# Half of a convolution inside the last units of the stage before it, a weight tile cleared in pieces, and eight input loads in advance

## What is computed

```python
x = x + einsum('bct,bcd->bdt', x, W0[condition])       # step 0, a 64x64 matrix per sample
x = x + conv1(x) * (t < len1[b])                       # step 1, causal, length 1024, per channel
x = x + x @ weight.T + bias + scale * lora(x)          # step 2, 1024x1024 over time, rank-16 adapter per sample
x = x + conv3(x * (t < len3[b])) * (t < len3[b])       # step 3, causal, as step 1
# the kernels of both convolutions: K[h, l] = 2 Re sum_n Ct[h, n] exp(dtA[h, n] * l)
```

## Time and profile before

| | us |
|---|---|
| median of three timed runs | 1580.62 |
| lowest and highest of them | 1577.86, 1584.58 |
| the profiled execution | 1581.37 |
| its span in the trace | 1579.6 |
| granted TensorE clock, mean | 0.984 |

### The profile page before, as it was taken

One profiled execution on the slowest core, in us unless ns is written; L12 is line 12 of the kernel. 1 busy time (PEld: TensorE's weight loads), 2 busy tenths in 40 slices (PEclk: granted clock), 3 DMA queues, 4 the chain that ended last, 5 costly groups with the idle time before them and its releaser, 6 DMA issues.

```text
span 1579.6 us, 36811 instructions
## 1 busy us (share of the span) xinstructions
PE 1496.6 (95%) x14983; PEld 1296.4 (82%) x14983; DVE 1238.7 (78%) x1478; ACT 744.0 (47%) x1084; POOL 636.6 (40%) x452
## 2 busy tenths in 40 slices
PE   6787777899999999999999999999999999999998
PEld 6687775778888888888888888888888888888887
DVE  7887757879696969696969787878878796969653
ACT  4544443345454545454535454545444444545433
POOL 2111122775444453535353535354545454545030
PEclk9999988999999999999999999999999999999999
DMA  7799985748493848567675747474849484848432
GB/s 226 274 356 381 360 332 174 173 94 224 93 222 98 210 118 193 135 173 155 153 175 132 196 116 201 109 206 110 215 89 231 88 227 82 234 94 224 101 134 68
DMA packets 437911, 283.43 MB, mean 179 GB/s; under 512 B 330568, under 2 KB 377168, under 8 KB 437776
## 3 DMA queue, kind: packets, MB, share of 16 engines
q1 hardware_dynamic: 388560, 172.47, 46.2%
q10 hardware_dynamic: 49216, 108.88, 19.9%
HBM read 159.20 MB, written 73.86 MB: 148 GB/s over the span
## 4 chain that ended last, share of the span: by engine, by line
PE 74%; DVE 9%; DMA 6%; issue 4%; ACT 3%; POOL 3%; ACTq 1%; DVEq 0%; POOLq 0%
PE ps L935 35%; PE ps L838 8%; PE ps L1023 6%; PE ps L944 5%; PE ps L911 5%; PE ps L882 4%; PE ps L1036 3%; DMA arena<-in_x_dram 3%; PE ps L848 3%; DVE arena L1839 3%; PE ps L786 3%; DMA w_scratch<-gbuf 1%; DVE gbuf L1834 1%; ACT arena L1380 1%; ACT arena L1287 1%
## 5 line engine op out<-in xcount | busy, mean ns | idle before, releaser
L935 PE MATMUL ps<-arena,w2t 128*128 128x256 f16 x4608 | 523.3, 273 | 5.9 <-DMA w2t<-w_scratch 4.7
L935 PEld LDWEIGHTS ps<-arena,w2t 128*128 128x128 f16 x4608 | 451.5, 98 | 62.8 <-DMA w2t<-w_scratch 5.0
L641 POOL TENSOR_TENSOR arena<-arena 128x68 f32<-128x68 f32 x31 | 26.6, 859 | 685.2 <-DVE arena L1889 394.1
L1932 DVE TENSOR_TENSOR arena<-arena 128x512 f16<-128x512 f32 x128 | 111.1, 869 | 115.8 <-ACT arena L1369 115.8
L786 PE MATMUL ps<-arena 128*128 128x128 f32 x1024 | 141.6, 300 | 44.0 <-DMA arena<-in_x_dram 23.5
L786 PEld LDWEIGHTS ps<-arena 128*128 128x128 f32 x1024 | 133.3, 212 | 50.1 <-DMA arena<-in_x_dram 27.1
L1356 ACT ACTIVATE arena<-ps,biasx 128x256 f32<-128x256 f32 x256 | 103.5, 472 | 137.0 <-PE ps L935 99.6
L1827 DVE SCALAR_TENSOR_TENSOR arena<-gbuf,arena 128x1024 f16<-128x1024 f32 x64 | 162.9, 2565 | 1.6 <-ACT arena L1283 1.6
L1369 ACT ACTIVATE arena<-arena 128x512 f16<-128x512 f32 x128 | 80.6, 630 | 163.3 <-DVE arena L1928 157.9
L882 PE MATMUL ps<-arena 128*128 128x512 f16 (+1 forms) x768 | 137.8, 330 | 7.8 <-DVE arena L1827 7.8
L1023 PE MATMUL ps<-arena 128*128 128x256 f16 (+1 forms) x1536 | 137.1, 246 | 1.9 <-DVE gbuf L1834 0.8
(11 more groups left out here) (255 smaller groups left out, 2777.9 us busy)
## 6 DMA issues: line engine op xcount, KB each, us to landing
w2t<-w_scratch ACTq DMA_DIRECT2D x96, 512.0 KB, 4.1
arena<-in_x_dram SPq DMA_DIRECT2D x64, 512.0 KB, 8.4
out_dram<-arena SPq DMA_DIRECT2D x64, 512.0 KB, 3.2
gbuf<-x_scratch SPq DMA_DIRECT2D x60, 512.0 KB, 5.6
x_scratch<-arena ACTq DMA_DIRECT2D x28, 960.0 KB, 11.0
gbuf<-w_scratch ACTq DMA_DIRECT2D x32, 512.0 KB, 4.2
arena<-krow_scratch SPq DMA_DIRECT2D x31, 512.0 KB, 8.5
arena<-tab_scratch SPq DMA_DIRECT2D x62, 68.0 KB, 2.2
```

Source lines behind the costliest of these rows:

```text
L935: mm = nc.tensor.matmul(ps[:, bank, n * HW:(n + 1) * HW], weight(p, n, part, k), xx[:, :, k], start=(fresh and n == 0 and k == 0 and q == ...
L1932: tt(x3_quarter(x3l, h0, row), x3part[slot].rearrange("p (k h b) -> p k h b", k=2, h=2), x3_quarter(x3h, h0, row), ALU.subtract).then_inc( ...
```

## The change

Stage 0's last units take in work of group 0's step 1. The input of blocks 0 to 3 (the first half of the times) is complete after unit 3; it is split in unit 6, and `near1` of the first half runs for the four heads in steps 4 to 7 of unit 7. Tables and bases of group 0 are made earlier, in new places. The rest of group 0's convolution is done by halves in another order. The opening clears `pick` in eight pieces on two engines, changes the order of loads, and loads eight x tiles ahead instead of four. The diff, cut:

```diff
+        x_ahead = area(104, 16).rearrange("p (s n t) -> p s n t", s=NXIN, n=GPAIRS)
+        def x_slot_free(i, l):
+            if i == 0 and l < 2 * NXIN:
+                return 0
+            back = 2 * NXIN if i == 0 and l < 3 * NXIN else NXIN
+            return 2 * STEPS * i + 2 * (l - back + 1)
...
+        FIRST_BANKS = ((4, 6, 5, 7), (2, 3, 5, 7))
 # SP
-            for n, row in enumerate((ids0, len1, ids2)):
-                sp.dma_start(ids[:, n, :], ...)
-            for quarter in range(4):                                  # w0
+            for half in range(2):                                     # w0 first
+            for n, row in ((1, len1), (2, ids2)):
+            sp.wait_ge(ssm_loaded, 160)
             stage0(NBLK // 2 - 1, False)
-            sp.wait_ge(x1_stored[0][NPART - 1], 16 * NBLK // 2)
             wait_u(0, 0)
             turn_u(0, 0)
 # POOL
             nc.gpsimd.iota(pcoli, ...)
+            for n in range(4):
+                nc.gpsimd.memset(pick[:, PAIRS // 2 + 8 * n:PAIRS // 2 + 8 * (n + 1), :], 0.0)
-            nc.gpsimd.memset(area(0, 32), 0.0).then_inc(pick_cleared, 1)
...
                 pool.wait_ge(u_made, n + 1)
+                if is_first(v, g):
+                    pool.wait_ge(tab_stored[0], 16 * NBLK // 2)
...
             pool.wait_ge(w_stored, 64 * NQ)
-            pool.wait_ge(tab_stored[0], 16 * NBLK // 2)
             make_tables(0, 0)
 # PE, stage0
+                        if blk == NBLK - 1 and step >= 4:
+                            near1_first(0, step - 4)
+            def near1_first(half, h):
+                if half == 0:
+                    wait g1_turned 1, x1_half_hi 1, x1_half_lo 1, k_scaled NBLK - 1, w2_hi NLOT, w2_lo NLOT
+                else:
+                    wait x1_hi h + 1, x1_lo h + 1, and the last copies (h < 2) or c1_half_out h + 1
+                for d in range(2):
+                    for q, (part, split) in enumerate([(0, 0), (0, 1), (1, 0)]):
+                        nc.tensor.matmul(o, g1[:, h, part, d * P:(d + 1) * P], m, ...)   # 512 columns, then 256
 # PE, after stage 0
-            near1(0, 0) ... far1(0, h)
+            states(0, 0, 0)
+            states(0, 0, 1)
+            for h in range(HG):
+                far1_first(0, h)
+            near1_first(1, 0)
+            near1_first(1, 1)
+            stage2(0, True)          # the first two blocks of 24 matmuls, from x2's first half
+            states(0, 0, 2)
+            near1_first(1, 2)
+            near1_first(1, 3)
+            for h in range(HG):
+                far1_first(1, h)
 # PE, stage2(0): the OWN blocks come ahead of low_products
 # ACT
+            act.dma_start(ids[:, 0, :], ids0...)                       # ahead of the parameters
-            act.wait_ge(pick_cleared, 1)
 # ACT, stage0: store_lot of the second lot ahead of the x1 store in step 2; store_tab(6) in step 1
+                    if step == 3 and blk == NBLK - 2:
+                        x1_half_split_hi()       # wait x1_kept 4; 128x2048 in one operation
+                    if step == 5 and blk == NBLK - 1:
+                        bases_hi(0, 0)           # wait u_made
 # ACT, after stage 0
-            bases_hi(0, 0)
+            table_hi(0, 0)
             copy_even(NBLK // 2 - 1, 2 * STEPS - 2)
             ... x1_kept_last
+            act.wait_ge(v_lo, 1)
+            state_hi(0, 0, 0)
+            x1_split_hi(0, 0), (0, 1)            # half a head each now
+            state_hi(0, 0, 1)
+            x1_split_hi(0, 2), (0, 3); x2_half_split_hi(0), (1)
+            state_hi(0, 0, 2)
+            x2_half_split_hi(2), (3)
 # DVE, opening
+            for n in range(4):
+                nc.vector.memset(pick[:, 8 * n:8 * (n + 1), :], 0.0).then_inc(pick_half_cleared, 1)
-            dve.wait_ge(iota_done, 3)
+            dve.wait_ge(iota_done, 1)
 # DVE, stage0
+                    if blk == NBLK - 2 and step == 3:
+                        turn_g1(0)
+                    if blk == NBLK - 2 and step == 6:
+                        x1_half_split_lo()
+                    if blk == NBLK - 1 and step == 6:
+                        bases_lo(0, 0)
 # DVE, after stage 0
+            table_lo(0, 0)
             copy_odd(...); keep_x1(...)
+            state_lo(0, 0, 0); x1_split_lo(0, 0), (0, 1)
+            state_lo(0, 0, 1); take_half(0, 0), (0, 1); x2_half_split_lo(0), (1)
+            x1_split_lo(0, 2), (0, 3); take_half(0, 2), (0, 3)
+            state_lo(0, 0, 2); x2_half_split_lo(2), (3)
+            take_half(1, 0), (1, 1); x2_split_lo(0, 0), (0, 1)
+            take_half(1, 2), (1, 3); x2_split_lo(0, 2), (0, 3)
```

More of the change, by code:

```diff
@@ L253, in build @@
         x_loaded = [sem(f"x_loaded{s}") for s in range(NXIN)]
+        x_ahead_loaded = [sem(f"x_ahead_loaded{s}") for s in range(NXIN)]
         s0_summed = sem("s0_summed")
@@ new lines, in far1_first @@
+            def far1_first(half, h):
+                bank = FIRST_BANKS[half][h]
+                n_states = NCH - 1 if half else 1
+                pe.wait_ge(st_hi[0], n_states)
+                pe.wait_ge(st_lo[0], n_states)
+                for d in range(2):
+                    for q, (part, ss) in enumerate([(0, 0), (0, 1), (1, 0)]):
+                        w, last = vd[0][:, part, h, d, :], d == 1 and q == 2
+                        if half:
+                            o = ps[:, bank, :].rearrange("p (k two b) -> p k two b", k=2, two=2)[:, :, d, :]
+                            mm = nc.tensor.matmul(o, w, st[0][ss][:, h, 1:3, :], start=False, stop=last)
+                        else:
+                            mm = nc.tensor.matmul(ps[:, bank, (2 + d) * B:(3 + d) * B], w, st[0][ss][:, h, 0, :], start=False, stop=last)
+                mm.then_inc(c1_summed if half else c1_half_summed, 1)
@@ L900, in far1, with stage2 @@
                 mm.then_inc(c1_summed, 1)
[L902 removed]
+            def stage2(g, opening=False):
                 first = isinstance(g, int) and g == 0
[L905 to L906 removed]
+                if not first:
+                    pe.wait_ge(x2_hi, HG * (g + 1))
+                    pe.wait_ge(x2_lo, HG * (g + 1))
                 products = [(0, x2h), (0, x2l), (1, x2h)]
@@ L971, in stage2 @@
                 for p in range(2):
-                    block(OWN_AT[p], p, resident(1), x2_quarter(0, NQ), True, False)
+                    if not first:
+                        block(OWN_AT[p], p, resident(1), x2_quarter(0, NQ), True, False)
                     delta(OWN_AT[p], p, 0, left_low, True).then_inc(s2_summed, 1)
@@ L1256, in stage0 @@
                     else:
-                        if step == 2:
+                        if step == 2 and blk < NBLK - 1:
                             store_tab(blk - 1, 1 - k)
@@ L1266, in stage0 @@
                             lot_hi(lots_of(blk - 1)[1])
-                        if step == 2 and lots_of(blk - 1)[1] is not None:
-                            store_lot(lots_of(blk - 1)[1])
                         if step == 7:
```

301 lines of the change are left out of this document (202 added, 99 removed).

## The result

| | before | after |
|---|---|---|
| median, us | 1580.99 | 1570.91 |
| lowest and highest of six runs | 1577.86, 1584.58 | 1567.56, 1574.91 |
| the profiled execution | 1581.37 | 1574.9 |
| its span in the trace | 1579.6 | 1572.9 |

The ratio is 0.9933, with a 95% interval of 0.9918 to 0.9948: 10 us gone, of 11 forecast. The profiled execution of the changed kernel is its slowest of the six; what slows it turned out to be the main lesson.

The account below looks back on a forecast made before the run. PE is busy 95% of the span; the end of the first stretch, limited by opening, DMA engines and seam, moves the whole kernel. Opening -3 and seam -8 make -11: 1580.6 to 1569.6, so 1570 us, 8-in-10 range 1562 to 1580.

Parts of the forecast that it names:

- The opening: Kernel start: split clearing, reordered loads and eight x loads ahead bring stage 0 earlier; -3 us (-6.4 to 0).
- Lots stored earlier: Step 2 of blocks: second lot's store ahead of x1 shortens ACT's stall; 0 us for the stage's end (to -2).
- POOL, start at 213, last product at 233: Unit 7: POOL's first table product near 213 us, after the last lot's store lands; its last near 233.
- The port lock: Unit 7: VectorE and GpSimd operations exclude each other; priced at 2 us on POOL's tables (0 to 5).
- The moved work: Units 6 and 7: splits, bases, near1_first and tables fit into existing waits and slack; cost 0 us (to +2).
- The seam: After stage 0: block 7's tables at 278.5 instead of 286.5 us, before the opening's gain; -8.0 us (-12 to 0).
- The table at 275.5 after the opening: Block 7's table (L1691) ends near 275.5 us; the prediction is wrong if it comes later than 281.
- (a): Rival at the seam: POOL's table comes 5 to 6 us later, seam gives 2 to 3 us; 1575.5 us, chance 0.20.
- (b): Rival: the opening is swallowed because bytes set stage 0's end; only the seam counts; 1572.6 us, chance 0.13.
- (c): Rival: the DMA-bound stretch gets denser as ACT no longer stalls; 2 to 5 us more, 1566 us, chance 0.08.
- (d): Rival: slower, ACT's bases_hi in unit 7 waits for POOL, holding copies; 1584 us, chance 0.07 with smaller mishaps.
- (e): Rival: the change does nothing because later stretches absorb it; chance 0.04.

Follow-up runs that it names:

- e3: The kernel before with only the change's opening, including eight x loads ahead: 1578.10 us, 0.9958 of the kernel before.
- e5: The kernel before with only the second lot's store moved ahead of the x1 store: 1580.96 us, 0.9985 of the kernel before.
- e11: The changed kernel with the second lot's store behind the x1 store again: 1573.40 us, 0.9943 of the kernel before.
- e2: The changed kernel with POOL waiting for DVE's last angles of block 7 before its tables: 1569.77 us, 0.9926 of the kernel before.
- e7: The changed kernel with POOL's six products of 1024 elements for group 0 cut in halves: 1566.96 us, 0.9891 of the kernel before.
- e8: The changed kernel with four x loads in advance instead of eight: 1571.87 us, 0.9927 of the kernel before.
- e12: The changed kernel with POOL's products in halves and ACT's weight load issued ahead of its wait for POOL's second table: 1567.78 us, 0.9908 of the kernel before.
- e9: The changed kernel, unaltered, measured and profiled again: 1571.44 us, 0.9935 of the kernel before.

## Why the prediction was right, point by point

The forecast of 1570 us met 1570.9, partly because errors cancelled.

- **What bounds the kernel**: held. From the table of block 7 to the end it is 1292.4 to 1295.0 us in every profile but one.
- **The opening, -3**: the ratios say -3 to -4 (-6.6 alone, e3). The parts of it were off both ways. Stage 0 begins 4.4 us earlier, not 2: the parameter chain started at 10.42 us, not at the 11.9 that I set by the last id load, and DVE's memsets took 0.91 us, my lower end. The eight loads gave nothing.
- **Lots stored earlier, 0 to -2**: -1 to -2 (e5 and e11), neither clear of the noise. The likeliest value should have been inside the range, not at its end: ACT's stall had copies behind it, and PE waited 4.6 us for one of them in the profile of before.
- **POOL, start at 213, last product at 233**: 208.15 and 223.08. It was early by 5 us at the start, and its tables took 16.2 us, not the 20 that I gave them with the lock. Its large products, from 210.30, so met DVE's chain of angles, from 211.31; in e2, where POOL started at 214.96, the seven operations escaped.
- **The port lock, 2 us (0 to 5), on POOL's tables**: this is the step that failed. I took the right rows and the right rule, and put the price on the wrong engine. I priced by the long DVE splits that doubled; the case in unit 7 is a chain of short ones, each of which waited out a whole product: 13.1 us for 2.4 us of work, on DVE, with PE's copy behind. The row that had this price was the other one, the cast of the earlier trace rows, which waited out a memset for 5.68 us and takes 0.53 in the changed kernel. POOL lost next to nothing. What cutting its products gives back: from 0.9933 to 0.9891 or 0.9888, 6.6 to 7.1 us across chips; on one chip 5.7 (e7 against e8), 4.3 (e12 against e9, where ACT's order differs too). I had 2, and 5 at the most. Since the seven still took 6.9 and 4.4 us in the cut versions, the lock's whole cost may be larger.
- **The moved work, 0 (to +2)**: for PE's own share the size was right. The near groups took 1.14 us each (4.6, against 4.4 worked out), between the groups of x matmuls. What the moved work costs in time was not measured by itself. "Wrong if PE waits in unit 7 for copies" was met, with 11.54 us, for the lock and not for the moved work.
- **The seam, -8.0**: 48.1 to 39.8, that is -8.3 in eight of eleven profiles. The ladder holds, within 1.5 us a step, in the profile above: opening blocks to 253.5 us (252.2 forecast), DVE's idle time 5.75 us (5.6) until 256.2 (255.7), last low half of x2 at 263.6 (262.9), table at 279.15 (278.5). These absolute times agree only because the lock gave back the opening's lead.
- **The table at 275.5 after the opening**: 279.15 and 273.07 in the two profiles of the changed kernel, on both sides of it. Both hold a chain of DVE caught by the lock; which chain it is, and so the cost, depends on where DVE stands when POOL's products begin.
- **PE's wait for w_scratch, 9 us expected**: 4.54, but with 3.79 us for ACT (L1490) ahead of it, a wait that the kernel before did not have there. Together 8.3 us: the size was right, the one name was not.
- **The rivals**: (a), that POOL's table holds the seam, happened where POOL was made to start late (e2: DVE idle for 5.9 us behind ACT's high half of the table), not in the changed kernel (1.05 us). (b) was wrong over repeated runs, though single traces spoke for it. (c), a denser bound stretch, is small: from 60 to 200 us 377 GB/s against 370, and from 200 to 230 us, with the lock's gap in it, 324 against 384. (d) did not happen in the first profile, where u was made at 216.7 us and ACT's `bases_hi` came at 229.90. In others ACT did wait there for u, 1.58 us in e9 and 7.33 us in e2; both kernels were faster than before all the same. (e), no effect, lies outside the interval of the ratio.

The sum with measured sizes: -3 to -4 for the opening, -1 to -2 for the order, +4 to +7 for the lock, and -10.6 in all (0.9933), leave -8.6 to -13.6 for the seam and the moved work. The 8.3 us that the traces show there are just short of its near end; whether the rest lies ahead of the last copy or in the parts' uncertainty stays open.

## What to carry to other kernels

Before you move GpSimd work beside a busy VectorE, list VectorE's short operations there that read SBUF, and price each at one whole GpSimd operation; then see whose copy stands behind the last. If the sum is large, cut the GpSimd operations: halves were enough here (4 to 7 us gained for 2 us of extra GpSimd time), and cutting did better than starting later by the medians, though not clear of the noise. And where the code up to a point is the same, look at that point in more than one profile before you explain a difference: here it strayed by 8 us.

## What the runs showed that I had not expected

- In unit 7 the lock falls on one side. POOL's products took 1.93 to 2.34 us beside DVE's chain, as without it, while DVE's of 0.28 to 0.43 us took 1.9 to 2.5. Each of them ended within 0.3 us after a product of POOL: 214.44 behind 214.29, 216.99 behind 216.71, 218.93 behind 218.77. So a chain of DVE moves at one operation for each of POOL's, however short it is.
- Elsewhere it falls on the other side. Later in the same profile a small product of POOL, 0.30 us when it ran alone at 208.41, stood beside two long splits of DVE (1.21 us from 300.97, then L1960), took 3.29 us and ended 0.2 us behind them. A short operation beside long ones of the other engine pays for their whole length, on whichever engine it is:

```profile
300.72 3.29 POOL L690 TENSOR_TENSOR arena<-arena 128x68 f32<-128x68 f32 x1
302.10 1.74 DVE L1960 SCALAR_TENSOR_TENSOR arena<-arena 128x1536 f16<-128x1536 f32 x1
```

- Four memsets of DVE took 0.91 us each beside four of POOL, which took 3.61 us without a gap (0.91 to 4.52 us): no lock is seen between these two, where the cast beside POOL's long memset took 5.68 us.
- The versions with halves and with quarters beat both kernels: 1567 us, 0.989 of the kernel before; the cheap way to the gain was to let an engine off the critical path take longer.
